# A Mamba block's rows of B by DMA out of DRAM, four decay banks, halved front steps and later silu sessions

## What is computed

```python
def mamba_block(x, in_proj_w, conv_w, conv_b, x_proj_w, dt_proj_w, dt_proj_b, A_log, D_skip, out_proj_w):
    xz = x @ in_proj_w
    xi, z = jnp.split(xz, 2, axis=-1)              # 256 channels each
    xi = silu(causal_conv4(xi) + conv_b)
    dbc = xi @ x_proj_w
    delta = softplus(dbc[..., :64] @ dt_proj_w + dt_proj_b)
    Bm, Cm = dbc[..., 64:80], dbc[..., 80:]        # 16 states each
    A = -jnp.exp(A_log)
    # for each position t:
    #   h = exp(delta_t * A) * h + (delta_t * xi_t) * B_t
    #   y_t = sum over the 16 states of h * C_t
    y = y + D_skip * xi
    return (y * silu(z)) @ out_proj_w
```

## Time and profile before

| | us |
|---|---|
| median of 3 runs | 1242.74 (1239.62 to 1247.82) |
| the profiled execution | 1240.69 |
| its span, first to last instruction | 1238.4 |
| Mamba block, to the end of its last DVE instruction | 174.5 |

### The profile page before, as it was taken

The page is one execution under the profiler, slowest core; times in us unless marked ns, Lnnn a source line. Parts: engine busy times, 40 slices in busy tenths (PEclk is TensorE's granted clock), DMA queues, the critical chain, the costliest instruction groups (busy, mean ns, idle before and its releaser), DMA issues. The chain is left out here.

```text
span 1238.4 us, 26336 instructions
## 1 busy us (share of the span) xinstructions
PE 1132.5 (91%) x9652; PEld 720.1 (58%) x9652; DVE 945.4 (76%) x1385; ACT 850.9 (69%) x1363; POOL 649.4 (52%) x522
## 2 busy tenths in 40 slices
...
DMA packets 75510, 107.11 MB, mean 86 GB/s; under 512 B 25347, under 2 KB 31938, under 8 KB 75002
## 3 DMA queue, kind: packets, MB, share of 16 engines
...
## 5 line engine op out<-in xcount | busy, mean ns | idle before, releaser
L1691 POOL TENSOR_TENSOR st_sq_sum<-h 128x512 f32<-128x512 f32 x96 | 122.1, 1272 | 224.0 <-ACT h L1448 223.2
L1695 POOL TENSOR_TENSOR mo_w<-mo_w,x 128x512 f32<-128x512 f32 x96 | 122.6, 1278 | 101.9 <-DVE x L1566 101.9
L1580 DVE SCALAR_TENSOR_TENSOR st_turned<-banks,mo_w 128x1024 f32<-128x1024 f32 x96 | 117.5, 1224 | 72.0 <-ACT banks L1459 38.6
L1448 ACT ACTIVATE h<-banks 128x512 f32<-128x512 f32 x192 | 114.5, 597 | 71.5 <-PE banks L1291 67.2
L1311 PEld LDWEIGHTS banks<-st_wv,stream 128*128 128x128 f32 x768 | 100.8, 192 | 45.1 <-issue 44.4
L1352 PEld LDWEIGHTS banks<-st_p_blocks,st_vs 128*64 128x64 f32 x1536 | 81.6, 137 | 78.0 <-issue 73.2
L1697 POOL TENSOR_TENSOR mo_w<-mo_w,x 128x512 f32<-128x512 f32 x96 | 122.5, 1276 | 0.0
L430 POOL TENSOR_TENSOR ma_dbx<-ma_u,ma_b_rows 128x1024 f32<-128x1024 f32 x32 | 75.4, 2357 | 76.0 <-ACT ma_b_rows L288 52.0
L1480 ACT ACTIVATE st_p_blocks<-banks 64x512 f32<-64x512 f32 x192 | 112.0, 583 | 3.2 <-PE banks L1340 0.8
L1704 POOL TENSOR_TENSOR mo_w<-st_prob,st_ri 128x512 f32<-128x512 f32 x96 | 100.4, 1046 | 15.0 <-DVE st_ri L1666 15.0
L1299 PE MATMUL banks<-st_sq_sum,head_ones 128*128 128x512 f32 x192 | 101.1, 609 | 6.9 <-POOL st_sq_sum L1691 6.8
...
## 6 DMA issues: line engine op xcount, KB each, us to landing
...
st_w_raw<-in_w_qk SPq DMA_DIRECT2D x12, 512.0 KB, 4.9
...
st_wv<-in_w_v SPq DMA_DIRECT2D x12, 256.0 KB, 3.0
st_wo<-in_wo SPq DMA_DIRECT2D x12, 256.0 KB, 3.0
```

What stands on the lines that cost most here:

```text
L1448: A(sq[:, part, :], ps[:, part, :], ACT.Square).then_inc(sq_done.sem, 1)
L1580: v.scalar_tensor_tensor(turned[:, h % 4], NORM_BANK.unsqueeze(1).to_broadcast([P, 2, SEQ]), 1e12, cos_part[:, which], ALU.min, ALU.mult). ...
L1691: nc.gpsimd.tensor_tensor(sq_sum[:], sq[:, 0, :], sq[:, 1, :], ALU.add).then_inc(sq_summed.sem, 1)
L1695: nc.gpsimd.tensor_tensor(cos_part[:, which, 0, :], cos_part[:, which, 0, :], sin_part[:, 1, :], ALU.subtract).then_inc(add_done.sem, 1)
```

## The change

The functions are the same and the barrier behind the block stays. The rows of B no longer go over PE and ACT: ACT copies the 16 rows of B of a batch to `b_flat`, SP writes them to a DRAM tensor (32 KB), waits for it, and then issues for each item a DMA that reads one row of 2 KB into all 128 partitions (256 KB), in a ring of four buffers; a load into a buffer waits for the POOL multiply of four items before. `spread_b`, `copy_b` and B_BANK are gone, and that bank (6) is the fourth for decays. `taps`, `in_w`, `rms_w` and `pick` are loaded from ACT's queue at its very start. PE runs 10 products of a zeroed bf16 tile ahead of the two means and 8 behind them (`busy`); there are none within the items. In the front, the gate products of batch 0 come behind the low rank product, softplus, delta, u and the first dbx are done by halves, and z is only copied out of its bank (`raw`). Silu comes in three later sessions of ACT, each between two table loads: xi of batch 1 behind decay(3), z of batch 0 behind decay(16), z of batch 1 behind decay(23). The gate products of batch 1 stand behind add_state(0) and add_state(1). The multiplies u = delta * xi of batch 1 (items 12 and 16) and silu(z) of batch 0 (behind item 19) go from DVE to POOL. At the end of batch 1 the skip, the multiply and the output product go by halves.

```diff
-    select = sb("select", [P, 2 * STATES, P], F32R)
+    select = sb("select", [P, STATES, P], F32R)
+    b_flat = sb("b_flat", [P, 2, SEQ])
...
-    DECAY, SPARE, SUM, B_BANK, C_BANK = (0, 1, 2), 3, 4, 6, 7
+    DECAY, SPARE, SUM, C_BANK = (0, 1, 2, 6), 3, 4, 7
...
+    BANK = dict(x00=2, x01=3, z00=4, z01=5, x10=3, x11=4, z10=3, z11=3)
...
+        for i in range(ITEMS):
+            b, n = divmod(i, STATES)
+            if n == 0:
+                sp.wait_ge(b_flat_done.sem, b + 1)
+                sp.dma_start(d["states"][b], b_flat[64:64 + STATES, b, :]).then_inc(b_out.sem, 16)
+                sp.wait_ge(b_out.sem, 16 * (b + 1))
+            if i >= B_RING:
+                sp.wait_ge(dbx_done.sem, 2 * (i - B_RING + 1))
+            sp.dma_start(b_rows[:, i % B_RING, :], bass.AP(d["states"].tensor, i * SEQ, [[0, P], [1, SEQ]])).then_inc(b_in[i % B_RING].sem, 16)
...
         def low_rank(b, bank):
-            pe.wait_ge(silu_done.sem, 4 * b + 2)
             for k in range(2):
+                pe.wait_ge(silu_done.sem, 2 * b + k + 1)
                 last = mm(ps[:, bank, :], proj_w[:, k, :], xc[:, b, k, :], start=(k == 0), stop=(k == 1))
...
+        pe.wait_ge(still_done.sem, 1)
+        busy(10)
         pe.wait_ge(C["x_in"][0].sem, 32)
         mean(0)
         mean(1)
+        busy(8)
...
         low_rank(0, 6)
+        gate_proj(0, 0)
         pe.wait_ge(dt_copied.sem, 1)
         pe.wait_ge(*ln_done.at(0, 2))
         for k in range(2):
             step_size(0, k, k)
         pe.wait_ge(select_done.sem, 1)
         pe.wait_ge(low_done.sem, 1)
-        spread_b(0)
         spread_c(0)
+        gate_proj(0, 1)
         pe.wait_ge(*hn_done.at(0, 2))
-        pe.wait_ge(silu_done.sem, 4)
-        convolved(1, 0, 4)
-        spread_b(1)
-        convolved(1, 1, 5)
-        for k in range(2):
-            gate_proj(1, k, 3 - k)
+        pe.wait_ge(silu_done.sem, 2)
+        convolved(1, 0)
+        pe.wait_ge(raw_done.sem, RAW["z00"])
+        convolved(1, 1)
         pe.wait_ge(C["const_in"].sem, C["const_n"])
         pe.wait_ge(out_in.sem, 16)
-        spread_b(2)
         for i in range(ITEMS):
-            if i + 3 < ITEMS:
-                spread_b(i + 3)
+            if i == 4:
+                pe.wait_ge(raw_done.sem, RAW["z11"])
+                low_rank(1, SPARE)
+            if i == 7:
+                pe.wait_ge(dt_copied.sem, 2)
+                pe.wait_ge(low_done.sem, 2)
+                pe.wait_ge(b_flat_done.sem, 2)
+                step_size(1, 0, SPARE)
+            if i == 11:
+                pe.wait_ge(delta_done.sem, 3)
+                step_size(1, 1, SPARE)
+            if i == STATES + 4:
+                pe.wait_ge(delta_done.sem, 4)
+                out_proj(0)
             if i + 1 < ITEMS:
                 spread_c(i + 1)
             add_state(i)
-            if i == 2:
-                pe.wait_ge(silu_done.sem, 8)
-                low_rank(1, SPARE)
-            if i == 4:
-                pe.wait_ge(dt_copied.sem, 2)
-                pe.wait_ge(low_done.sem, 2)
-                step_size(1, 0, SPARE)
-            if i == 8:
-                pe.wait_ge(delta_done.sem, 2)
-                step_size(1, 1, SPARE)
-            if i == STATES + 2:
-                out_proj(0)
+            if i in (0, 1):
+                pe.wait_ge(raw_done.sem, RAW[("x10", "z10")[i]])
+                gate_proj(1, i)
...
+        ac.dma_start(in_w[:], d["in_w"]).then_inc(front_in.sem, 16)
+        ac.dma_start(taps[:].rearrange("p i k c -> p (i k c)"), bass.AP(d["taps"].tensor, 0, [[0, P], [1, 8 * P]])).then_inc(front_in.sem, 16)
+        ac.dma_start(rms_w[:], d["rms1"]).then_inc(front_in.sem, 16)
+        ac.dma_start(pick[64:128], d["pick"]).then_inc(pick_in.sem, 16)
...
+        def raw(which):
+            to = (xc if which[0] == "x" else sz)[:, int(which[1]), int(which[2]), :]
+            ac.wait_ge(front_done.sem, FRONT[which])
+            A(to, ps[:, BANK[which], :], ACT.Copy).then_inc(raw_done.sem, 1)
...
-        def copy_b(i):
-            ac.wait_ge(b_done.sem, i + 1)
-            if i >= 3:
-                ac.wait_ge(dbx_done.sem, i - 2)
-            A(b_rows[:, i % 3, :], ps[:, B_BANK, :], ACT.Copy).then_inc(b_copied.sem, 1)
+        def flat(b, bank):
+            A(b_flat[64:64 + STATES, b, :], ps[64:64 + STATES, bank, :], ACT.Copy).then_inc(b_flat_done.sem, 1)
 
         def decay(i):
             b, n = divmod(i, STATES)
-            if n == 0:
-                ac.wait_ge(delta_done.sem, 1 + 2 * b)
             for k in range(2):
                 j = 2 * i + k
-                if j >= 3:
-                    ac.wait_ge(scan_done.sem, j - 2)
-                A(ps[:, DECAY[j % 3], :], delta[:, b, k, :], ACT.Exp, scale=a_neg[:, k, n:n + 1]).then_inc(decay_done.sem, 1)
-
-        def softplus(k):
-            ac.wait_ge(dtp_done.sem, 3 + k)
-            A(mag[:, 1, k, :], ps[:, SPARE, :], ACT.Abs).then_inc(softplus_step.sem, 1)
-            ac.wait_ge(softplus_step.sem, 4 + 3 * k)
-            A(mag[:, 1, k, :], mag[:, 1, k, :], ACT.Exp, scale=-1.0).then_inc(softplus_step.sem, 1)
-            ac.wait_ge(softplus_step.sem, 5 + 3 * k)
-            A(mag[:, 1, k, :], mag[:, 1, k, :], ACT.Ln, bias=C["one"]).then_inc(softplus_step.sem, 1)
+                if n == 0:
+                    ac.wait_ge(delta_done.sem, 2 * b + k + 1)
+                if j == 2:
+                    ac.wait_ge(silu_done.sem, 1)
+                if j == 3:
+                    ac.wait_ge(low_done.sem, 1)
+                if j >= 4:
+                    ac.wait_ge(scan_done.sem, j - 3)
+                A(ps[:, DECAY[j % 4], :], delta[:, b, k, :], ACT.Exp, scale=a_neg[:, k, n:n + 1]).then_inc(decay_done.sem, 1)
...
+        def activated(which, at):
+            nc.scalar.preload_act_table_set("silu_and_others")
+            ac.wait_ge(raw_done.sem, RAW[at])
+            if which == "x1":
+                for k in range(2):
+                    A(xc[:, 1, k, :], xc[:, 1, k, :], ACT.Silu, bias=chan[:, k, 0:1]).then_inc(silu_done.sem, 1)
+            else:
+                b = int(which[1])
+                A(sz[:, b], sz[:, b], ACT.Silu).then_inc(silu_done.sem, 1)
+            nc.scalar.preload_act_table_set("natural_log_exp_and_others")
 
         high(0, 6)
-        ac.wait_ge(dtp_done.sem, 2)
-        A(mag[:, 0], ps[:, 0:2, :], ACT.Abs).then_inc(softplus_step.sem, 1)
-        ac.wait_ge(softplus_step.sem, 1)
-        A(mag[:, 0], mag[:, 0], ACT.Exp, scale=-1.0).then_inc(softplus_step.sem, 1)
-        ac.wait_ge(softplus_step.sem, 2)
-        A(mag[:, 0], mag[:, 0], ACT.Ln, bias=C["one"]).then_inc(softplus_step.sem, 1)
-        copy_b(0)
+        flat(0, 6)
+        magnitude(0, 0)
+        decline(0, 0)
+        magnitude(0, 1)
+        log_of(0, 0)
+        decline(0, 1)
+        log_of(0, 1)
         ac.wait_ge(a_step.sem, 2)
         decay(0)
-        copy_b(1)
-        nc.scalar.preload_act_table_set("silu_and_others")
-        silu(1, 4, (3, 2))
-        nc.scalar.preload_act_table_set("natural_log_exp_and_others")
-        ac.wait_ge(silu_done.sem, 8)
-        copy_b(2)
+        raw("z00")
+        raw("z01")
         for i in range(1, ITEMS):
             decay(i)
-            if i + 2 < ITEMS:
-                copy_b(i + 2)
-            if i == 4:
+            if i == 1:
+                raw("x10")
+                raw("x11")
+            if i in (2, 3):
+                raw(("z10", "z11")[i - 2])
+            if i == 3:
+                activated("x1", "x11")
+            if i == 7:
                 high(1, SPARE)
-            if i == 7:
-                softplus(0)
-            if i == 11:
-                softplus(1)
+                flat(1, SPARE)
+            if i in (10, 13):
+                magnitude(1, i // 13)
+                decline(1, i // 13)
+            if i in (11, 14):
+                log_of(1, i // 14)
+            if i == 16:
+                activated("z0", "z01")
+            if i == 23:
+                activated("z1", "z11")
...
-        dv.wait_ge(softplus_step.sem, 3)
-        v.scalar_tensor_tensor(delta[:, 0], ps[:, 0:2, :], 0.0, mag[:, 0], ALU.max, ALU.add).then_inc(delta_done.sem, 1)
-        dv.wait_ge(delta_done.sem, 1)
-        dv.wait_ge(silu_done.sem, 2)
-        v.tensor_tensor(u[:, 0], delta[:, 0], xc[:, 0], ALU.mult).then_inc(u_done.sem, 1)
+        for k in range(2):
+            step_sizes(0, k)
+            dv.wait_ge(delta_done.sem, k + 1)
+            dv.wait_ge(silu_done.sem, k + 1)
+            v.tensor_tensor(u[:, 0, k, :], delta[:, 0, k, :], xc[:, 0, k, :], ALU.mult).then_inc(u_done.sem, 1)
         for i in range(ITEMS):
             scan(i, 0)
             if i >= 1:
                 times_c(i - 1)
             scan(i, 1)
-            if i == 4:
-                split(1, SPARE)
-            if i == 8:
-                step_sizes(0)
-            if i == 12:
-                step_sizes(1)
-            if i == STATES:
-                gate(0)
```

(50 more changed lines are left out.)

98 lines of the change are left out of this document (49 added, 49 removed).

## The result

The changed kernel took 1225.6 us (median of 4 runs, 1221.8 to 1227.8) against 1242.7 of before; the ratio is 0.9855, 95% interval 0.9813 to 0.9898. The profiled execution took 1224.2 us with a span of 1222.4. The forecast was 1220 for an execution and 1222 for the median: 20.6 us less than before. The medians fell by 17.1.

The account below looks back on a forecast made before the run. DVE's 3.36 us per item bounds the Mamba block, plus waits. Front 30.4, items 104.2, other DVE work 5.7, waits 6.5 and end 7.1 make 153.9 against 174.5, so 1220 us (median 1222), range 1211 to 1231.

Parts of the forecast that it names:

- the loop over B: Within the items: PE's spread of B, ACT's copy, decay and DVE's scan wait on each other; the change cuts this.
- Front, (a): Front, up to the convolution's start: earlier loads from ACT's queue bring it from 11.1 to 10.0 us.
- (b): Front, convolution start to low rank product done: 12.9 becomes 8.9 us, with PE at the high clock level by 7.
- (c): Front, low rank product to scan(1, 0), the first scan of item 1: 16.0 becomes 11.5 us through halved steps.
- P: Time in the front at which the low rank product is done; the steps up to scan(1, 0) are counted from it.
- Other DVE work: DVE operations in the block that no item needs: 10.1 becomes 5.7 us, as multiplies move to POOL.
- Waits within the items: Waits within items 1 to 31: 11.0 becomes 6.5 us, of which 4.0 is a stall at item 4.
- the one for item 3: Within the items: item 3's decays stand behind the raw copy of z10, a wait of 0.4 us.
- End of the block: From the last scan to the block's end: 9.2 becomes 7.1 us by working in halves.
- The clock did not stay low over many items: Rival, chance 0.2: PE's clock sinks within the items; 1228 us with ten low stretches, 1246 if low in all 31.
- Rows of B were never late: Rival, chance 0.03: B's rows arrive late from DRAM, making the kernel slower; loads bind from 11 us, 1258 at 16.
- 0.62, 0.06, 0.09 and two thirds of 0.2: Chances of: as summed (1220), no stall at item 4 (1214), front gives little (1226), clock sinks within the items (1228).

Follow-up runs that it names:

- b_dma_alone: Kernel before with only the rows of B sent over DRAM in a ring of four, without spread and copy of B; 1232.0 us, block end 165.2.
- z_late: Changed kernel with batch 1's gate products moved behind items 13 and 14; 1218.1 us, ratio to before 0.980, block end 148.3.
- sp_loads: Changed kernel with the loads of in_w, taps, rms_w and pick issued by SP again; scan(1, 0) at 32.0, block end 158.0 us.
- after_again: Changed kernel, unaltered, profiled a second time; scan(1, 0) at 32.0, block end 158.0 us, 1068.0 us behind it.
- on_dve: Changed kernel with batch 1's two u multiplies and batch 0's multiply with silu(z) back on DVE; block end 162.6 us.
- no_products: Changed kernel without the 18 products of the zeroed tile in the front; scan(1, 0) at 31.9, block end 154.4 us.
- three_banks: Changed kernel with three decay banks instead of four; scan(1, 0) at 31.6, block end 154.0 us.
- ring1: Changed kernel with one buffer for the rows of B instead of four; block end 215.1 us, 5.5 us an item.
- z_late_plain: Changed kernel with batch 1's gate products behind items 13 and 14, three decay banks, two B buffers, no zeroed-tile products; 1219.0 us, ratio 0.9797, block end 150.7.

## Why the prediction was right, and where it was off

The direction, the size and the main mechanism held: 153.9 forecast for the block, 155.3 and 158.0 measured; 1220 for an execution and 1222 for the median, 1224.2 and 1225.6 measured, inside the range. The block shrank by 18.8 us on average over two executions each, where 20.6 was forecast. That the loop over B made the waits is shown by b_dma_alone, that the copies ahead of the session made the stall by z_late. Some terms came out well by luck, as said below.

- **Front, (a), was mis-sized**: convolution at 10.0 forecast, 10.65 and 11.13 measured. The weights came even earlier than I took (multiply at 6.98 against 7.9), with the loads moving at 319 GB/s and not at the 248 of the sum. The Trainium skill (Trainium Kernel Development and Optimization, Key Constraints) says that several issuers save only issue time; sp_loads agrees, with 2.1 us at the weights, under the 3 us of issues. But I gave the earlier issue as a gain without asking what it delays: x came 1.8 us later, which by itself held up hn little, hn waited 0.50 us for `rn`, and `pick` came 2.2 us later, which put POOL's cast beside the first hn (1.80 us in place of 0.75). I had looked for POOL beside DVE only at u.
- **(b)** 8.9 forecast, 9.05 measured (10.65 to 19.70). PE was at the high level for the second mean (1.13 for two passes at 7.41).
- **(c)** 11.5 forecast, 11.9 measured, in part by errors that cancel. The row of B released the first dbx at P + 6.3 (6.7 forecast). u of half 1 met the dbx and took 1.76 in place of 0.69, the 1.1 us that stood as "up to 1.2" outside the sum; POOL waited 0.62 us for it. In after_again DVE's u came 0.08 us ahead of the dbx and took 0.69, and the dbx took 1.74 in place of 1.27: 11.8 all the same. By the rule of the Trainium skill (SBUF — State Buffer, Who interferes with whom), by which the two contend, something for this belonged inside the sum; both executions agree with it.
- **Other DVE work** 5.7 forecast. 31.56 to 148.06 (the end of scan(31, 1)) is 116.5; less 104.2 and 7.2 of waits leaves 5.1. on_dve put the moved multiplies at 4.3 to 4.5, where the sum had 4.4.
- **Waits within the items** 6.5 forecast, 7.2 and 9.5 measured. The term that failed is the one for item 3, put at 0.4: it was 1.73 and 3.08. PE had waited 3.05 us for times_c(0) and add_state(0) ran at the low level (3.28 and 3.78 us in place of 1.98), which the forecast allowed for item 4 only. In the two executions where the clock did not sink there (no_products, three_banks), item 3 did not wait and item 4 waited 3.89, as the sum has it. Item 4 at 3.80 (4.0) is no separate hit in the first profile: its decay came 1.7 us later than forecast, and the wait at item 3 had moved the scan by the same. times_c(5) waited 1.33 and 2.14 (1.8), and z_late showed the cause of all three. Item 12 waited 0.36 (0.3).
- **End of the block** 7.1 forecast, 7.2 measured.
- **Behind the barrier** nothing was forecast, which holds on average. But the sum was made against an execution that was lucky there by 3.3 us (1063.9 against a mean of 1067.2), and the 2 us between it and the median were all that I added for it.
- **Rivals.** The clock did not stay low over many items (1.00 in 60 to 75 and again from 95 on), but it sank in 75 to 85, at no cost. Rows of B were never late behind item 0, and ring1 prices them: 3.1 us is far from binding with four buffers. With two (z_late_plain) dbx waited for its row in seven items, and still no scan did. The chances for "faster" do not add up as written: 0.62, 0.06, 0.09 and two thirds of 0.2 make 0.90 and not 0.88.
- Of the parts of the change, the fourth bank and a ring of more than two buffers are worth nothing that shows in the time. B over DRAM gives half of the gain or somewhat more (9.3 and 11.1); the three multiplies on POOL (two u and the gate's) give 4.5.
